# Attention scores as f32 products in four row groups, with the factorization's steps at new places

## The reference, cut to what matters

```python
h = modulate(layernorm(x), shift_msa, scale_msa)          # x: (16, 128, 144)
q, k, v = heads(h @ W_qkv + b_qkv)                         # 16 heads of 9
o = softmax((q * 9**-0.5) @ k.T) @ v
x = x + gate_msa * (o @ W_proj + b_proj)
x = x + gate_mlp * (gelu(modulate(layernorm(x), ...) @ W_fc1 + b_fc1) @ W_fc2 + b_fc2)
U, _ = qr(P)                                               # P: (144, 64)
R = expm(A)                                                # A: skew, 64 x 64 per batch, from the condition
z = x @ U;  x = x + (z @ R - z) @ U.T
```

## Time and profile before

| | |
|---|---|
| median of three executions | 365.78 us |
| profiled execution: its time | 364.83 us |
| its span, first to last instruction | 363.0 us |
| mean granted clock of TensorE | 0.951 of 2.4 GHz |
| busy: TensorE products | 320.1 us, 88% |
| busy: TensorE weight loads | 244.1 us, 67% |
| busy: VectorE | 254.1 us, 70% |
| busy: ScalarE | 187.9 us, 52% |
| busy: GpSimd | 130.9 us, 36% |

### The profile page before, as it was taken

The page is one execution under the profiler, slowest core; times in us unless marked ns, Lnnn a source line. Parts: engine busy times, 40 slices in busy tenths (PEclk is TensorE's granted clock), DMA queues, the critical chain, the costliest instruction groups (busy, mean ns, idle before and its releaser), DMA issues.

```text
span 363.0 us, 10511 instructions
## 1 busy us (share of the span) xinstructions
PE 320.1 (88%) x3919; PEld 244.1 (67%) x3919; DVE 254.1 (70%) x1064; ACT 187.9 (52%) x403; POOL 130.9 (36%) x389
## 2 busy tenths in 40 slices
PE   0698899889989899999999999999987769999995
PEld 0472569567777787878877877777865553556784
DVE  7472046688999989878696788988898646443243
ACT  1222454356957657568576686786642314623221
POOL 3622134235455355454453444645543410000000
PEclk9988965789999999999999999999999989999999
DMA  8705100000000000000000000000000000000013
GB/s 206 221 9 195 69 1 2 3 1 4 0 3 4 2 5 2 2 2 3 2 5 0 5 2 2 3 3 0 4 1 5 0 3 0 2 0 2 0 34 99
DMA packets 8542, 8.17 MB, mean 22 GB/s; under 512 B 1011, under 2 KB 8090, under 8 KB 8364
## 3 DMA queue, kind: packets, MB, share of 16 engines
q1 hardware_dynamic: 7784, 6.67, 6.2%
q10 hardware_dynamic: 708, 0.83, 0.8%
HBM read 6.29 MB, written 1.20 MB: 21 GB/s over the span
## 4 chain that ended last, share of the span: by engine, by line
PE 62%; DVE 17%; ACT 9%; issue 5%; POOL 4%; DMA 2%; ACTq 1%; DVEq 0%
PE bank L1239 5%; PE bank L1471 4%; PE bank L1302 4%; PE bank L1268 4%; PE bank L1455 4%; PE bank L1155 3%; PE bank L1257 3%; PE bank L1292 3%; PE bank L1284 3%; PE bank L1228 3%; PE bank L1229 2%; PE bank L1163 2%; PE bank L1258 2%; ACT KT L611 2%; PE bank L1247 2%
## 5 line engine op out<-in xcount | busy, mean ns | idle before, releaser
L436 POOL TENSOR_TENSOR root<-rec,mhalf 128x1 f32<-128x1 f32 x64 | 34.6, 540 | 105.1 <-DVE Z L907 105.0
L969 DVE TENSOR_REDUCE nmax<-bank 128x4 f32<-128x512 f32 x64 | 43.0, 672 | 32.9 <-PE bank L1247 32.6
L601 ACT ACTIVATE E<-bank 128x512 f32<-128x512 f32 x64 | 38.0, 594 | 39.0 <-PE bank L1258 38.6
L611 ACT ACTIVATE KT<-bank 64x512 bf16<-64x512 bf16 x64 | 37.5, 587 | 0.8
L1257 PE MATMUL bank<-QT,KT 128*128 128x128 bf16 x256 | 36.3, 222 | 0.0
L1258 PE MATMUL bank<-NMT,headsel 128*128 128x128 bf16 x256 | 35.8, 220 | 0.0
L1292 PE MATMUL bank<-Z,sel 128*128 128x128 f32 x128 | 29.2, 311 | 7.0 <-DVE Z L913 6.8
L1268 PE MATMUL bank<-E,V 128*32 128x128 f32 x512 | 27.5, 287 | 5.4 <-ACT E L601 5.3
L607 ACT ACTIVATE QT<-bank 128x512 bf16<-128x512 bf16 x32 | 19.0, 595 | 24.6 <-PE bank L1239 24.6
L1292 PEld LDWEIGHTS bank<-Z,sel 128*128 128x128 f32 x128 | 20.5, 197 | 15.0 <-issue 14.6
L1257 PEld LDWEIGHTS bank<-QT,KT 128*128 128x128 bf16 x256 | 24.1, 98 | 9.7 <-issue 9.7
(11 more groups left out here) (268 smaller groups left out, 824.5 us busy)
## 6 DMA issues: line engine op xcount, KB each, us to landing
gates<-gates_dram SPq DMA_DIRECT2D x1, 2304.0 KB, 8.4
x_all<-in_x_dram SPq DMA_DIRECT2D x4, 288.0 KB, 7.4
out_dram<-x_all SPq DMA_DIRECT2D x8, 144.0 KB, 2.0
wskew<-in_L_cond_W_dram SPq DMA_DIRECT2D x4, 283.5 KB
...
wproj<-in_L_cond_W_proj_dram SPq DMA_DIRECT2D x16, 5.1 KB
```

What stands on the lines that cost most here:

```text
L436: link(nc.gpsimd.tensor_tensor(root[:, at], rec[:, at], mhalf[:, 0:1], ALU.pow))
L601: nc.scalar.activation(E[:, q, :, :].rearrange("p i t -> p (i t)"), bank[4][:, :], ACT.Exp).then_inc(s_E, 1)
L611: nc.scalar.activation(KT[parity][n][own, p, :, :].rearrange("p g t -> p (g t)"), bank[2][own, 256:512].bitcast(BF16), ACT.Copy).then_inc( ...
L969: nc.vector.tensor_reduce(nmax[:, q % 2, 4 * (q // 2):4 * (q // 2) + 4], bank[3][:, :].rearrange("p (i m) -> p i m", i=4), AX.X, ALU.max, ...
```

## The change

The data of a head stays in f32. q, k and V are copied from the qkv product into slots of 32 columns (48 for V), four heads side by side fill 128 columns, and `stack_T` turns such a group into four heads on four groups of 32 rows. `scores` then has eight f32 products per half batch (eight heads), over nine rows each, head r of a group on rows 32r and into bank r. VectorE takes the maximum of all eight heads at once, 1024 elements per row, and writes minus the maximum into column 9 of the slot of q. The queries are transposed a second time with it (`queries_again_T`), the keys have a one there, and so `scores_T` is one product of ten rows per head. The same columns of banks 0 to 3 serve the scores and the transposed scores of both halves. The exponential is taken on 1024 elements at a time.

The product with V has a one as tenth column, so that the sum of the weights comes with it. The result is transposed back to time on partitions (`heads_back`), divided there on VectorE by a 16-wide reciprocal, transposed again (`normalized_T`), copied by ScalarE, and projected by two products.

The steps of the factorization (`STEPS`) stand now in all four quarters of b = -2 and -1, and then in three of an odd b and in four of an even one; the last still ends at b = 16. A step takes its one-hot matrix from a broadcast column of the identity; the selectors go. All stages of the generator's exponential come one batch later (`POWER, HALVES, ODD, SQUARE = 3, 6, 7, 8`), the norms and the scaling in b = 2 and the check in b = 3 rather than all in b = 1, and all windows of the generator stand at the end of b = -1 and b = 0, not between the steps. Statistics and addition of batch b-2 move to the first quarter of the next slot. The splitting into bf16 parts, its selectors and its memsets are removed. Seventeen small loads of `W_proj` become three. `row_bank(k, b)` waits until steps k-1 (G) and k-2 (B) are done.

The order of ScalarE in a slot becomes: queries again (b-1), modulated (b+1), Osb (b-2), q, k and V into slots (b+1), exponential of half 0 (b-1), keys and queries copied (b+1), a stage of the generator, the normalized output copied (b-2), exponential of half 1 (b-1).

The order of VectorE: quarter 0 maximum of half 0, elimination, statistics; quarter 1 elimination, division; quarter 2 maximum of half 1, elimination, normalization, generator; quarter 3 elimination (if any), gating.

The diff, cut to its core:

```diff
-bank = [ctx.enter_context(nc.psum_tensor(f"bank{i}", [128, 512], F32)) for i in range(8)]
+banks = ctx.enter_context(nc.psum_tensor("banks", [128, 8, 512], F32))
...
-ATTENTION = (-2, B + 2, B + 1, B + 1)
+STEPS = {}
+for b in range(-2, B + 1):
+    for q in range(4):
+        if len(STEPS) <= RD and (b < 0 or q < 3 or b % 2 == 0):
+            STEPS[b, q] = len(STEPS)
+assert len(STEPS) == RD + 1
...
+def scored(n):
+    return banks[:, 0:4, 0:256]
...
-    for i in range(4):
-        for q in range(4):
-            sp.dma_start(wproj[32 * i:32 * i + D, q, :], wp[i, q // 2, q % 2, :, :]).then_inc(s_ldp, 16)
-    sp.dma_start(wproj[D:D + 1, 0, :], b_proj.rearrange("(a n) -> a n", a=1)).then_inc(s_ldp, 16)
+    sp.dma_start(wproj1[:, :], W_proj[0:C1, :]).then_inc(s_ldp, 16)
+    sp.dma_start(wproj2[0:C2, :], W_proj[C1:C, :]).then_inc(s_ldp, 16)
+    sp.dma_start(wproj2[C2:K2, :], b_proj.rearrange("(a n) -> a n", a=1)).then_inc(s_ldp, 16)
...
     def added(b):
-        wait(pool, s_pr, b + 2, s_apart[0])
-        xb = x_all[:, bass.ds(b, 1), :].rearrange("p a c -> p (a c)")
-        nc.gpsimd.tensor_tensor(xb, xb, tmp[:, :], ALU.add).then_inc(s_x1, 1)
+        pool.wait_ge(s_pr, b + 1)
+        nc.gpsimd.tensor_tensor(x_all[:, b, :], x_all[:, b, :], tmp[:, :], ALU.add).then_inc(s_x1, 1)
...
+    def keys_copied(b):
+        act.wait_ge(s_kT, b + 1)
+        wait(act, s_ST, 2 * b - 4)
+        nc.scalar.activation(KT[b % 3][:, :, :].rearrange("p j t -> p (j t)"), bank[5], ACT.Copy).then_inc(s_KT, 1)
+    def queries_copied(b):
+        act.wait_ge(s_qT, b + 1)
+        wait(act, s_S, 2 * b)
+        nc.scalar.activation(QT[:, :, :].rearrange("p j t -> p (j t)"), bank[4], ACT.Copy).then_inc(s_QT, 1)
+    def queries_again(b):
+        act.wait_ge(s_qmT, b + 1)
+        wait(act, s_ST, 2 * b)
+        nc.scalar.activation(QM[:, :, :].rearrange("p j t -> p (j t)"), bank[5], ACT.Copy).then_inc(s_QM, 1)
+    def stacked(b):
+        act.wait_ge(s_qkv, b + 1)
+        wait(act, s_qmT, b - 1)
+        wait(act, s_kT, b)
+        def per_head(which):
+            return bank[4][:, C * which:C * which + C].rearrange("p (h d) -> p h d", h=H)
+        nc.scalar.activation(qstk[b % 2][:, :, 0:D], per_head(0), ACT.Copy, scale=SCALE).then_inc(s_stk, 1)
+        nc.scalar.activation(kstk[:, :, 0:D], per_head(1), ACT.Copy).then_inc(s_stk, 1)
+        wait(act, s_pv, 2 * b - 4)
+        nc.scalar.activation(V[b % 3][:, :, VO:VO + D], per_head(2), ACT.Copy).then_inc(s_V, 1)
+    def exponentials(b, g):
+        act.wait_ge(s_ST, 2 * b + g + 1)
+        wait(act, s_pv, 2 * b - 1 + g)
+        nc.scalar.activation(E[:, g, :, :, :].rearrange("p r j t -> p r (j t)"), scored(g), ACT.Exp).then_inc(s_E, 1)
...
-        dve.wait_ge(s_O, b + 1)
-        dve.wait_ge(s_div, b + 1)
-        TT(ON[:, :, :].rearrange("p q t -> p (q t)"), Osb[:, :], bank[6][:, :], ALU.mult).then_inc(s_on, 1)
+        dve.wait_ge(s_Ot, b + 1)
+        wait(dve, s_OnT, b)
+        slots = bank[7][:, 256:512].rearrange("p (h s) -> p h s", h=H)
+        link(nc.vector.reciprocal(rsum[:, :].rearrange("p (h a) -> p h a", a=1), slots[:, :, D:D + 1]))
+        TT(ON[:, :].rearrange("p (h d) -> p h d", h=H), slots[:, :, 0:D],
+           rsum[:, :].rearrange("p (h a) -> p h a", a=1).to_broadcast([128, H, D]), ALU.mult).then_inc(s_on, 1)
...
+    def maximum(b, g):
+        dve.wait_ge(s_S, 2 * b + g + 1)
+        wait(dve, s_qmT, b - 1)
+        nc.vector.tensor_reduce(qstk[b % 2][:, 8 * g:8 * g + 8, D:D + 1].rearrange("p (j r) a -> p r (j a)", r=4),
+                                scored(g).rearrange("p r (j m) -> p r j m", j=2),
+                                AX.X, ALU.max, negate=True).then_inc(s_max, 1)
...
+    def stack_T(dst, stack, done):
+        for j in range(4):
+            ins = pe.transpose(dst[:, 128 * j:128 * j + 128], stack[:, 4 * j:4 * j + 4, :].rearrange("p h s -> p (h s)"),
+                               ident[:, :])
+        ins.then_inc(done, 1)
+    def keys_T(b):
+        pe.wait_ge(s_stk, 2 * b + 2)
+        wait(pe, s_QM, b - 1)
+        if b == 0:
+            pe.wait_ge(s_v, 3)
+        stack_T(bank[5], kstk, s_kT)
+    def queries_T(b):
+        pe.wait_ge(s_stk, 2 * b + 2)
+        pe.wait_ge(s_V, b + 1)
+        stack_T(bank[4], qstk[b % 2], s_qT)
+    def queries_again_T(b):
+        pe.wait_ge(s_max, 2 * b + 2)
+        stack_T(bank[5], qstk[b % 2], s_qmT)
+    def scores(b, g):
+        pe.wait_ge(s_QT, b + 1)
+        pe.wait_ge(s_KT, b + 1)
+        wait(pe, s_max, 2 * b + g)
+        wait(pe, s_E, 2 * b - 2 + g)
+        if b == 0:
+            pe.wait_ge(s_v, 4)
+        for j in range(2):
+            for r in range(4):
+                rows = slice(32 * r, 32 * r + D)
+                ins = mm(bank[r][:, 128 * j:128 * j + 128], QT[rows, 2 * g + j, :], KT[b % 3][rows, 2 * g + j, :],
+                         start=True, stop=True)
         ins.then_inc(s_S, 1)
-    def scores_T(q, b, parity):
-        wait(pe, s_NMT, b + 1)
-        wait(pe, s_E, 4 * b + q)
-        for i in range(4):
-            dst = bank[4][:, 128 * i:128 * i + 128]
-            mm(dst, KT[parity][q // 2][:, q % 2, i, :], QT[parity][q // 2][:, i, :], start=True, stop=False)
-            ins = mm(dst, headsel[:, q % 2, 4 * (q // 2) + i, :], NMT[:, :], start=False, stop=True)
+    def scores_T(b, g):
+        pe.wait_ge(s_QM, b + 1)
+        pe.wait_ge(s_max, min(2 * b + 3 + g, 2 * B))
+        wait(pe, s_E, 2 * b + g)
+        for j in range(2):
+            for r in range(4):
...
+    def values(b, g):
+        pe.wait_ge(s_E, 2 * b + g + 1)
+        if g == 0:
             wait(pe, s_O, b)
             pe.wait_ge(s_V, b + 1)
-        for i in range(4):
-            own, cols = slice(32 * i, 32 * i + 32), slice(128 * q, 128 * q + 128)
-            ins = mm(bank[5][own, cols], V[parity][:, head(q, i), :], E[:, q, i, :], start=True, stop=True)
+            if b == 0:
+                pe.wait_ge(s_L, 1)
+        weights = V[b % 3][:, :, :].rearrange("p h s -> p (h s)")
+        for p in range(2):
+            for i in range(4):
+                own, cols = slice(32 * i, 32 * i + 32), slice(128 * g, 128 * g + 128)
+                first = VS * (8 * g + 2 * i + p) + (0 if p else VO)
+                ins = mm(bank[6][own, cols], weights[:, first:first + 32], E[:, g, 2 * (i % 2) + p, i // 2, :],
+                         start=(p == 0), stop=(p == 1))
         ins.then_inc(s_pv, 1)
...
+    def heads_back(b):
+        pe.wait_ge(s_O, b + 1)
+        wait(pe, s_pr, b)
+        for n in range(2):
+            cols = slice(128 * n, 128 * n + 128)
+            ins = pe.transpose(bank[7][:, 256 + 128 * n:384 + 128 * n], Osb[:, cols], ident[:, :])
+        ins.then_inc(s_Ot, 1)
+    def normalized_T(b):
+        pe.wait_ge(s_on, b + 1)
+        pe.transpose(bank[5][:, 0:128], ON[:, 0:C1], ident[:, :])
+        pe.transpose(bank[5][0:C2, 128:256], ON[:, C1:C], ident[:, :]).then_inc(s_OnT, 1)
     def projection(b):
-        pe.wait_ge(s_on, b + 1)
-        for q in range(4):
-            ins = mm(bank[6][:, 0:C], ON[:, q, :], wproj[:, q, :], start=(q == 0), stop=(q == 3))
-        ins.then_inc(s_proj, 1)
+        pe.wait_ge(s_oT, 2 * b + 2)
+        mm(bank[7][:, 256:256 + C], oT1[:, :], wproj1[:, :], start=True, stop=False)
+        mm(bank[7][:, 256:256 + C], oT2[:, :], wproj2[:, :], start=False, stop=True).then_inc(s_proj, 1)
+    def step(b, q, before=None):
+        k = STEPS.get((b, q))
+        if k is not None or before:
+            last = k if k is not None else max([n for at, n in STEPS.items() if at < (b, q)]) + 1
+            row_bank(last, b)
+        if before:
+            before(b - 2)
+        if k is None:
+            return
+        if k < RD:
+            mm(bank[7][:, 0:2 * RD], ident[:, k:k + 1].to_broadcast([128, 128]), Z[:, 0:2 * RD],
+               start=True, stop=True).then_inc(s_Grow, 1)
+        if k > 0:
+            mm(bank[7][:, 2 * RD:3 * RD], ident[:, k - 1:k].to_broadcast([128, 128]), Z[:, 2 * RD:3 * RD],
+               start=True, stop=True).then_inc(s_Brow, 1)
...
+    def attention(b):
+        if scoring(b):
+            scores(b, 0)
+        if b >= 3:
+            pe.wait_ge(s_pr, b - 2)
+        step(b, 0)
+        if closing(b):
+            values(b - 2, 1)
+        if b == B + 1:
+            transposed_again(0)
+        if prepares(b):
+            qkv(b + 1)
+        if b == -1:
+            generator_entries(3, 4)
+        if weighing(b):
+            scores_T(b - 1, 0)
+        step(b, 1, heads_back if closing(b) else None)
+        if b == B + 1:
+            transposed_again(1)
+        if prepares(b):
+            keys_T(b + 1)
+            queries_T(b + 1)
+        if b == B:
+            U_parts(b, 0)
+        if scoring(b):
+            scores(b, 1)
+        if weighing(b):
+            values(b - 1, 0)
+        generator_stage(b)
+        if b == B:
+            U_parts(b, 1)
+        if closing(b):
```

(32 more changed lines are left out.)

659 lines of the change are left out of this document (237 added, 422 removed).

## The result

The changed kernel takes 426.85 us (median of 4, 421.7 to 430.0), the kernel before 366.14 beside it (4, 364.4 to 367.1): **15.7% slower, ratio 1.157 (1.151 to 1.163)**. The forecast was 358.5, with a range up to 373. The profiled execution took 430.0, the longest of the four; its span is 428.2.

The account below looks back on a forecast made before the run. TensorE's instruction stream was taken to set the pace, VectorE right behind. Start +10.1, b=2 to b=15 -11 and tail -6.5 summed to -7.4, so 358.5 us from a median of 365.78; range 342 to 373.

Parts of the forecast that it names:

- rival (4): Inside the batches the clock falls, pulled down by waits for a third of each: +21, 379 us; chance 0.05.
- The rule on transposes: Twenty f32 transposes per batch would make rival (4) likelier; the prediction held that earlier trace rows disagree; no size given.
- The allowance at a change of form, 0.17: TensorE's score phases: 0.17 us at the change of form, taken as what a drain costs, nothing more added.
- 0.67 for eight score products: TensorE's score phases: two rounds of four row groups, 0.5 us, plus 0.17; bounds 0.5 and 2.0.
- TensorE's sum, 9.4 per batch: TensorE's work in a new batch adds up to 9.4 us, against 11.8 in the old one.
- the batch of 11.9: Plain batch: walked at 11.6 us mean, taken as 11.9 with small hand-offs, 1.0 less than 12.9.
- Rival (3): TensorE's score phases: row groups don't overlap at 128 columns, +73, 430 us; chance 0.03.
- rival (2): Shared score banks and eliminations keep batches at 12.9, or the start costs more: 372 us, deciding from 12.4; chance 0.2.
- VectorE's walk in b=2 to 7: Generator work lies in VectorE's chain, adding +1.1 to +3.3 in priced batches; 85 us for the six.
- The start, +10.1: Up to b=2: b=-2 +6 and b=-1 +8 with eight early steps, b=1 -3.4; together +10.1 us.
- The windows, priced at 6 for the first block: b=-1: 64 windows, 3.9 us before, take 6 at the lower clock.
- The tail, -6.5: From the start of b=16 to the M products: 14.9 us instead of 21.5, -6.5; -3 if half comes.

Follow-up runs that it names:

- e1: The changed kernel with the transposed scores contracting over all 32 rows of each group rather than 10; 405.5 us, ratio 1.109.
- e3: The changed kernel with all four score phases of a batch over 32 rows per group, GpSimd clearing the column of the maxima; 394.8 us, ratio 1.083.
- p1: The changed kernel plus ten wait-free TensorE streams behind its end: full products, row-group products of 9 or 32 rows, f32 transposes (stream 3); no kernel time given.
- e12: e8 plus windows spread over b=0, useless products in the tail, generator sums (b=4, 5) and joining of halves (b=6) behind the second maximum; 364.2 us, ratio 0.992.
- e8: e5 with the turned output in bank 4 rather than bank 5 in b=2 and b=7; 377.4 us, ratio 1.037.
- e5: e3 with the factorization's steps back at four in each of b=0 to 15, none in b=-2 and -1; 387.5 us, ratio 1.050.

## Why the prediction was wrong

**The step that failed** is the one that isn't in the sum: every duration was taken at TensorE's full clock, as the earlier trace rows read 1.00 in the middle. The clock was treated as a property of the run. It belongs to what TensorE streams, and the change took away 48 bf16 score products of 128 rows a batch (54 of the rows carry a score, as the description says; the instruction streams all) and put 32 of 9 and 10 rows in their place. That the new ones let it fall is shown (e1, e3, p1); that just those 48 had held it is inferred. The case stood as rival (4), with a chance of 0.05, a price of 21 us, and waits as its cause. Measured: 61 us in all, 32 of them by rows (e3), which no part of the prediction names. The clock also fell in the sum's own stages: b=1 was forecast at 15, took 20.9 at a clock of 0.58, and takes 15.7 at 0.84 in e3, which differs by the rows and one small memset.

**The rule on transposes** (the Trainium skill, TensorE: Matmul & The Clock Gate, Part 4: transposes don't bring the clock up). This case disagrees, and the earlier trace rows had it right: stream 3 of p1 climbs from 0.50 to 1.00. But holding to that argument closed the question of the clock for the wrong reason: the products next to the transposes were the ones to ask about. The prediction counts twenty f32 transposes in a batch; its own list has eighteen.

**The allowance at a change of form, 0.17.** The Trainium skill, TensorEngine Tiling (Array Packing), Key Properties, says that a change of tiling mode drains TensorE. The sum let its 0.17 stand for that, and its 0.67 for eight score products met the 0.66 measured, with two terms that were off by a little each way. In p1, where no form changes, the granted clock is 1.00, the instructions of two stretches are (count, ns of one, first to last start):

```profile
L1532 PE MATMUL banks<-KT,QT x152: 270/270/270, 437.3 to 441.5; 9*128 9x128 f32 x152
...
L1532 PE MATMUL banks<-KT,QT x440: 270/270/270, 497.8 to 510.0; 32*128 32x128 f32 x147
```

An instruction starts every 0.028 us, so eight products (sixteen instructions) take 0.445, with 9 rows as with 32, where the sum had 0.5. In the kernel the same eight take 0.66. So 0.22 more is paid among full-array products. The trace agrees with the drain that the page names, but no run shows what the 0.22 is made of.

**TensorE's sum, 9.4 per batch, and the batch of 11.9.** Rival (3) is out: row groups run side by side at 128 columns. Where the clock is full, the batch nearly came. The first qkv product of b=12, 13 and 14 in e1, which keeps the changed kernel's steps, at a granted clock of 1.00:

```profile
270.26 0.99 PE L1195 MATMUL banks<-wqkv,hT 128*128 128x432 f32 x2
...
282.92 0.99 PE L1195 MATMUL banks<-wqkv,hT 128*128 128x432 f32 x2
...
294.47 0.99 PE L1195 MATMUL banks<-wqkv,hT 128*128 128x432 f32 x2
```

That is 12.66 for a batch with four steps and 11.55 for one with three, 12.1 in the mean, against 11.9 forecast, 12.9 before and 15.8 in the changed kernel (b=12 and 13). With a squaring e1 takes 13.4 and 14.8, 14.1 in the mean, against 13.2 forecast and 15.0 before. So with the clock held the change is worth 0.8 to 0.9 us in such a batch, and rival (2), whose point is 12.4, is not met there; its other case, that the start costs more, did come. A plain batch with four steps at full clock, TensorE in order of time, e12:

```profile
228.25 0.99 PE L1200 MATMUL banks<-wqkv,hT 128*128 128x432 f32 x2
...
234.78 0.73 PE L1253 MATMUL banks<-QM,KT 32*128 32x128 f32 x16 [0.30 <-issue]
236.32 0.48 PE L1296 MATMUL banks<-wproj,oT 128*128 128x144 f32 x2 [0.81 <-DVE Z L821]
236.73 0.51 PE L1297 MATMUL banks<-wproj,oT 17*128 17x144 f32 x2
237.17 0.49 PE L1310 MATMUL banks<-Z,ident 128*128 128x128 f32 x2
...
239.75 0.49 PE L1310 MATMUL banks<-Z,ident 128*128 128x128 f32 x2 [0.61 <-DVE tmp L834]
```

By distances of starts: qkv 1.65 (forecast 1.53), four score phases 2.64 (2.68), values 1.15 (1.2), twelve transposes 1.41 (1.3), the small ones 0.82 (0.7), four row steps 1.97 (1.54 for 3.5), projection 0.85 (0.5): 10.5. The 17-row product of the projection costs as much as the 128-row one. With some 2 us of waiting the batch is 12.65 (e12, b=12 and 13), with a squaring 14.6. So in e12, where every batch has four steps again, only 0.3 to 0.4 us of a batch is left; the rest came with the half step less. The waits stand where rival (2) put them, before the rows and the projection of the second half.

**VectorE's walk in b=2 to 7.** Priced at +1.1 to +3.3 per batch for operations, but not for what TensorE has queued behind: bank 5 (4.1 us in b=2, 3.2 in b=6 and in b=7) and the maximum behind the generator's sums (1.5 in b=4 and b=5). The six batches were forecast at 85; they took 113.5, with 32 rows 104.8 (e3), with the waits mended 90.6 (e12), and 86.6 before.

**The start, +10.1.** It was +23.3 (104.9 against 81.6). The eight steps ahead of b=0 cost 13 to 16 there (e3 against e8 and e5), where the sum had 14 for b=-2 and -1, windows included. At full clock the half step less saves 0.5 us a batch (12.1 against 12.65), an estimated 8 in all, so the early steps don't pay. Waiting for VectorE's walk, 10.8 us up to 110, was in it; the clock behind those waits wasn't. The windows, priced at 6 for the first block, took 13.7 in both.

**The tail, -6.5.** It didn't come: 114.9 against 111.1 from b=14 on, with the clock at 0.50 from 340 to 360. From the factorization's last row to the M products the kernel before takes 19.8, the changed one 19.6 at a clock of 0.50, and e3 17.4 at 0.81, so 2.5 of the 6.5 are there at the least when the clock is higher.
